# Loading the rows for the scatters in pairs of token tiles, in a two-layer transformer with routed experts

## The chip, the core and the metric

The kernel runs on one core of a Trainium2 chip. The metric is the device time of one execution in microseconds (us); lower is better.

## The reference

The input is x, 4 sequences of 1024 tokens with 256 features in float32. Two layers follow. In each, the same normalised rows go to an attention part and a feed-forward part, and both results are added to x:

```python
xn = _layernorm(x)
x = x + L0_attn(xn) + L0_ffn(xn)
xn = _layernorm(x)
x = x + L1_attn(xn) + L1_ffn(xn)
```

Layer 0 has causal softmax attention and a dense ReLU network. Layer 1 has gated attention in groups of 64 tokens with a linear part beside it, and eight experts:

```python
scores = softmax(xf @ Wg.T)
expert_weights, expert_indices = top_k(scores, 2)
g = silu(h1) * h3                  # h1, h3: each expert's own matrices, with a low-rank part
y_e = _lora_out(g, W2, b2, A2, B2)
y = einsum('te,ted->td', gates, y_e)
```

Each of the 4096 tokens uses the two experts with the highest scores, and the kernel computes only those.

## The kernel before, in words

The program has four stages, joined on every engine: layer 0 (to about 465 us), attention of layer 1 for the first two sequences (to about 620 us), the experts for all tokens (to about 970 us), attention of layer 1 for the last two sequences together with the adding of the experts' results. TensorE works in all of them. Tokens are handled in 32 tiles of 128.

**The rows of the experts.** Layer 0 leaves in HBM (xn1_scratch, `scr["xn1"]`) for every token two copies of its normalised row, each followed by the gate of one of its experts: 2 x 257 floats, 2056 bytes for each token. When every token's experts are known, VectorE works out for each token and choice a slot (unit CH, the last of it at L1734), such that the slots of one expert are contiguous, 71 tiles of 128 slots in all. Then the rows must be moved to their slots in slot_rows_scratch (`scr["xs"]`). That takes two steps for each tile of tokens. SyncE loads the tile into one place of `ring` in SBUF, which has RINGS = 4 places of one tile (unit RG, L1303). GpSimd then issues two scatters by index, one for each choice (unit SC, L1347). The semaphore `ring_in` of the place tells GpSimd that the load has landed; the semaphore `moved` of the place, raised by 16 by each scatter that has landed, tells SyncE that the place is free (L1302). So RG:n waits for both scatters of tile n - 4. When all is moved, SyncE loads the slots' rows, six tiles ahead, into xs_ring (unit ML, L1830 to L1833), and the experts' stage begins (units MR, MA, MC, MG, MO for every tile of slots: rows turned, two products, gate, turned again, product out).

**What else stands in the same queues.** The order of units on each engine is written out by hand (ATTENTION_UNITS, L1007), and an engine never departs from it. GpSimd's has the 32 SC, and among them YS:0 to YS:8, each the power -0.5 of one tile's variance (L1339), and LE:0 to LE:2, the three parts of the first expert's matrices (L1783 and L1787; LE:1 stands between SC:26 and SC:27, LE:2 between YS:8 and SC:29). YS:9 and those after it stand behind SC:31. YS:n waits for VectorE's variance (L1679) of the same tile; VectorE's unit YF:n (L1683, L1688) waits for YS:n, finishes that tile's normalised output and adds it to x1b. YF:9 stands right behind OO:15, the last product with the gate (L1668), and ahead of the statistics of tiles 11, 12 and 13 (YS), which the first unit of the experts follows (MR:0, L1989). SyncE's queue has, among its RG: SX:n, which stores four finished tiles of x1b (L1295), and LX:1, which loads the second sequence's residual rows, 1024 KB, into x1b once the first is stored (L1288 to L1290, the load itself at L1166). XB:1 on VectorE (L1650) needs those. AHEAD (L1076) says how many units of the next stage are taken in right behind a unit of this one: on SyncE twelve behind RG:31, which are ML:0 to ML:5 and the first six MT, so SX:2 and SX:3 come behind these.

In the views below, tile names are the program's: `slot_rows_scratch<-ring,slot` is a scatter, `ring<-xn_scratch` a load of the ring, `x1b<-x_scratch` LX, `x_scratch<-x1b` SX, `expert_ring<-experts_scratch` a part of an expert, `rsy<-vey,half` YS.

Of the kernel before, what the change touches and what calls it, by code (L numbers as in the profile page):

```python
# [13 lines left out]
P = 128  # L14
# [251 lines left out]
def layer0(nc, io, keep, scr, psum, ctx):  # L266
# [725 lines left out]
    def bank_last(i):  # L992
# [40 lines left out]
        SC:28 YS:8 LE:2 SC:29 SC:30 SC:31 YS:9 YS:10 YS:11 YS:12 YS:13 YS:14 YS:15  # L1033
    """,
    "sync": """
        LC:0 LC:1 LX:0 LC:2 RG:0 RG:1 RG:2 RG:3 RG:4 RG:5 RG:6 RG:7 RG:8 RG:9 RG:10 RG:11 RG:12 RG:13 RG:14 RG:15
        RG:16 RG:17 RG:18 RG:19 RG:20 RG:21 RG:22 RG:23 RG:24 RG:25 SX:0 RG:26 RG:27 SX:1 RG:28 LX:1 RG:29 RG:30
        RG:31 SX:2 SX:3
    """,
},  # L1040
{
# [44 lines left out]
    "scalar": "GA:15:18",  # L1086
    "vector": "YS:13:1 YS:14:2 YF:11:1 YS:15:4 YF:12:19 YF:13:1 YF:15:2",
    "gpsimd": "YS:10:1 YS:13:1",
    "sync": "RG:31:12",
},  # L1090
{
    "tensor": "MC:70:1",
# [76 lines left out]
def attention(nc, io, keep, scr, psum, half, out, ctx, before):  # L1169
# [39 lines left out]
    if half:  # L1209
        z_in, z_stored = [sem(f"first_half_in{b}") for b in range(NB)], sem("first_half_stored")  # L1210
        added = {n: [sem(f"added_{n}_{t}") for t in range(4)] for n in ("z", "x")}
    else:
        chosen, slots_ready, ranks_ready = sem("experts_chosen"), sem("slots_ready"), keep["ranks_ready"]
        w_in, c_in, row_in = sem("l1_weights_in"), sem("l1_cols_in"), sem("l1_rows_in")
        spread_ready, rowprod, folded = sem("ln1_bias_spread"), sem("l1_bias_products"), sem("l1_folded")
        w_high, w_split, offset_step = sem("l1_weights_high"), sem("l1_weights_split"), sem("head_offsets_step")
        ring_in = [sem(f"ring_in{i}") for i in range(RINGS)]
        moved = keep["moved"]
    x2_b = scr["x2"].rearrange("(b t p) d -> b p t d", p=P, t=TPB)
    out_b = out.rearrange("b (t p) d -> b p t d", p=P)  # L1220
# [37 lines left out]
    def sync(sp):  # L1258
        def unit(un):
# [10 lines left out]
            elif kind == "LC" and n == 1:  # L1270
                for read in dense["probs_turned"]:
                    sp.wait_ge(*read)
                sp.dma_start(turn[:], io["turn"]).then_inc(row_in, 16)
                sp.wait_ge(*dense["rows_weighed"])
                sp.dma_start(wo1[:], io["L1_attn_Wo"].rearrange("(c p) n -> p c n", p=P)).then_inc(keep["late_in"], 16)
            elif kind == "LC" and n == 2:
                sp.wait_ge(*dense["columns_read"])
                sp.wait_ge(*dense["crow_read"])
                sp.dma_start(keep["bias"][:], io["distance_bias"]).then_inc(keep["late_in"], 16)
                sp.wait_ge(*dense["hidden_read"])  # L1280
                sp.dma_start(keep["ln2_w"][:], io["L1_attn_ln2_w"].to_broadcast([P, DIM])).then_inc(keep["late_in"], 16)
                sp.dma_start(keep["ln2_b"][:], io["L1_attn_ln2_b"].to_broadcast([P, DIM])).then_inc(keep["late_in"], 16)
            elif kind == "LX" and (n or half == 0):
                if half == 0 and n == 0:
                    sp.wait_ge(*dense["hidden_read"])
                    dense["x1_rows"](sp, BATCH - 1)
                elif half == 0:
                    for h in range(2):  # L1288
                        sp.wait_ge(stored[h], 16)
                load_rows(sp, keep, scr, "x", half, n, x[n][:])  # L1290
            elif kind == "SX":
                b, rows_of = n // 2, slice(n % 2 * 4, n % 2 * 4 + 4)
                sp.wait_ge(x_ready, T0 + 4 * n + 4)
                to = out_b[b + NB] if half else x2_b[b]
                sp.dma_start(to[:, rows_of, :], x[b][:, rows_of, :]).then_inc(stored[n], 16)  # L1295
            elif kind == "RG":
                if n == 0:
                    for b in range(2, BATCH):
                        dense["stored"](sp, b)
                    sp.wait_ge(*dense["gates_stored"])  # L1300
                if n >= RINGS:
                    sp.wait_ge(moved[n % RINGS], 32 * (n // RINGS))  # L1302
                sp.dma_start(ring[:, n % RINGS, :], scr["xn1"][n * P:(n + 1) * P].rearrange("p k d -> p (k d)")  # L1303
                             ).then_inc(ring_in[n % RINGS], 16)
            elif kind == "LZ":
                if n == 0:
                    sp.wait_ge(*before["rows_out"])
                    before["experts_in"](sp)
                sp.dma_start(zx[:, n, :, :], x2_b[n]).then_inc(z_in[n], 16)
            elif kind == "EN":  # L1310
                for q4 in range(2 * NB):
                    sp.wait_ge(stored[q4], 16 * (half + 1))
                sp.wait_ge(z_stored, 16 * 2 * NB)
            elif kind == "SZ":
                b, rows_of = n // 2, slice(n % 2 * 4, n % 2 * 4 + 4)
                for t in range(4 * n, 4 * n + 4):
                    sp.wait_ge(*all_added("z", t))
                sp.dma_start(out_b[b][:, rows_of, :], zx[:, b, rows_of, :]).then_inc(z_stored, 16)
# [3 lines left out]
    def gpsimd(pool):  # L1322
# [12 lines left out]
        def unit(un):  # L1335
# [5 lines left out]
            elif kind == "SC":  # L1341
                if n == 0:
                    pool.wait_ge(slots_ready, 1)
                    pool.wait_ge(*dense["cleared"])
                pool.wait_ge(ring_in[n % RINGS], 16 * (n // RINGS + 1))
                for k in range(TOPK):
                    nc.gpsimd.indirect_dma_start(out=scr["xs"], out_offset=index(k, n),  # L1347
                                                 in_=ring[:, n % RINGS, k * ROW:(k + 1) * ROW],
# [813 lines left out]
```

## Time and profile before

| | us |
|---|---|
| median of three runs | 1117.2 |
| lowest and highest of them | 1113.53 and 1121.52 |
| the profiled execution | 1116.3 |
| its span, from the first to the last instruction | 1114.6 |
| its mean granted TensorE clock | 0.974 of full speed |
| TensorE busy | 1055.8 (95%) |
| VectorE busy | 781.8 (70%) |
| GpSimd busy | 434.6 (39%) |
| ScalarE busy | 393.5 (35%) |
| loads of the ring: 32 issues of 257 KB | 466.4 to 596.0 |
| scatters: 64 issues | 486.6 to 606.2 |

All times in what follows count from the start of the profiled span. Busy shares are means over the whole of it; what a change in one stage is worth has to be read in that stage. A transfer counts as busy for nobody: its issuing engine goes on at once, and who needs the data waits on a semaphore. An idle time is written in brackets behind the instruction that ended it, with what the profile infers to have released it; "issue" is time in which the engine waited for nothing that the profile shows.

### The profile page before, as it was taken

How to read it: one execution, taken by the hardware profiler on the slowest of the kernel's cores; microseconds unless marked ns; L12 is line 12 of the kernel's file. 1: busy time of each engine (PE TensorE's matmuls, PEld its weight loads, DVE VectorE, ACT ScalarE, POOL GpSimd, SP SyncE). 2: the span in 40 equal slices, each digit the busy share in tenths (PEclk: the TensorE clock that was granted, in tenths of full speed). 3: DMA queues.
4: the chain of work that ended last, by engine and by line, in shares of the span. 5: the costliest groups of instructions: out<-in, count | busy, mean ns of one | idle time of the engine just before them, and what ended most of it. 6: DMA issues, size and time to landing. Idle time of an engine off the chain costs nothing.

```text
span 1114.6 us, 20433 instructions
## 1 busy us (share of the span) xinstructions
PE 1055.8 (95%) x6338; PEld 915.2 (82%) x6338; DVE 781.8 (70%) x1741; ACT 393.5 (35%) x770; POOL 434.6 (39%) x416
## 2 busy tenths in 40 slices
PE   5999999999999996995899899999999999999995
PEld 4899999999999996864677788888888888877874
DVE  5688787878788676754565777777777777764745
ACT  2636463555446363431211222222222222442300
POOL 2846454555447331045575100000011010088886
PEclk8999999999999998897899999999999999999998
DMA  9364672666468346425466446534355252265456
GB/s 272 97 206 130 187 244 101 192 160 202 140 190 205 123 148 185 126 76 171 151 189 214 166 136 223 171 116 142 101 194 166 78 194 58 84 123 86 68 95 141
DMA packets 113780, 168.61 MB, mean 151 GB/s; under 512 B 17296, under 2 KB 87568, under 8 KB 113552
## 3 DMA queue, kind: packets, MB, share of 16 engines
q1 hardware_dynamic: 93328, 120.09, 35.5%
q0 software_dynamic: 20352, 47.23, 15.3%
q8 instruction: 58, 0.95, 0.4%
q14 instruction: 42, 0.34, 0.1%
HBM read 96.14 MB, written 71.14 MB: 150 GB/s over the span
## 4 chain that ended last, share of the span: by engine, by line
PE 87%; DVE 4%; issue 2%; another core or an unknown queue 2%; DMA 2%; SPq 1%; POOL 1%; ACT 0%; DVEq 0%; POOLq 0%; ACTq 0%
PE wide L549 19%; PE wide L1900 17%; PE bank L549 11%; PE bank L1900 9%; PE wide L1398 7%; PE bank L1398 3%; PE bank L1925 3%; PE wide L1458 3%; PE wide L1482 2%; PE bank L1482 2%; PE bank L640 1%; PE bank L1893 1%; PE wide L1471 1%; PE wide L1468 1%
## 5 line engine op out<-in xcount | busy, mean ns | idle before, releaser
L1900 PE MATMUL wide<-expert_ring,xsT 128*128 x642 | 170.5, 401 | 3.1 <-DVE xsT L1989 2.3
L1900 PEld LDWEIGHTS wide<-expert_ring,xsT 128*128 128x128 f32 x642 | 113.3, 188 | 23.4 <-issue 3.9
L1958 ACT ACTIVATE gsT<-bank 128x512 fp32r<-128x512 f32 x71 | 42.5, 599 | 242.3 <-PE bank L1925 242.3
L1783 POOL DMA_DIRECT2D expert_ring<-experts_scratch x24 | 17.3, 720 | 264.7 <-issue 137.6
L2001 DVE TENSOR_TENSOR slots_h<-wide,expert_bias 128x512 f32<-128x512 f32 x71 | 49.1, 691 | 68.0 <-PE wide L1900 67.8
L1347 POOL DMA_INDIRECT slot_rows_scratch<-ring,slot x64 | 69.2, 1081 | 52.0 <-DVE slot L1734 32.0
L532 POOL TENSOR_TENSOR folded_matrix<-fold,folded_matrix 128x512 fp32r<-128x512 f32 x48 | 64.0, 1341 | 42.5 <-ACT folded_matrix L726 39.7
L549 PE MATMUL wide<-xnT,w 128*128 128x512 f32 x234 | 60.3, 399 | 0.0
L1900 PEld LDWEIGHTS bank<-expert_ring,gsT 128*128 128x128 f32 x432 | 56.1, 189 | 3.5 <-issue 0.3
L944 DVE TENSOR_TENSOR hT<-hid,hT 128x512 fp32r<-128x512 f32 x64 | 54.6, 860 | 5.9 <-ACT hid L781 5.1
L549 PE MATMUL wide<-xnT,pT 128*128 128x512 f32 (+2 forms) x288 | 58.6, 348 | 0.0
L529 POOL TENSOR_TENSOR rsa<-vea,half 128x1 f32<-128x1 f32 x32 | 21.3, 666 | 95.3 <-DVE vea L908 94.3
L1900 PE MATMUL bank<-expert_ring,xsT 128*128 x210 | 57.5, 409 | 0.1
L1900 PE MATMUL bank<-expert_ring,gsT 128*128 x432 | 57.3, 281 | 0.1
L1900 PEld LDWEIGHTS wide<-expert_ring,gsT 128*128 128x128 f32 x420 | 54.2, 188 | 3.0
L1989 DVE TENSOR_TENSOR gsT<-bank,gsT 128x512 fp32r<-128x512 f32 x71 | 49.1, 691 | 9.9 <-ACT gsT L1958 0.5
L549 PE MATMUL wide<-w,hT 128*128 128x256 f32 x456 | 55.7, 278 | 0.0
L1330 POOL DMA_INDIRECT first_half<-slot_results_scratch,slot x32 | 51.9, 1622 | 9.2 <-issue 9.2
L1900 PE MATMUL wide<-expert_ring,gsT 128*128 x420 | 55.2, 280 | 0.0
L2010 DVE SCALAR_TENSOR_TENSOR slots_g<-slots_h,xs_ring,slots_h 128x512 f32<-128x512 f32 x71 | 53.4, 752 | 2.5
L549 PEld LDWEIGHTS wide<-w,hT 128*128 128x128 f32 x456 | 54.5, 188 | 0.4
L1330 POOL DMA_INDIRECT x1b<-slot_results_scratch,slot x16 | 26.0, 1626 | 73.4 <-DVE x1b L1650 68.9
(284 smaller groups left out, 2589.1 us busy)
## 6 DMA issues: line engine op xcount, KB each, us to landing
experts_scratch<-folded_matrix SPq DMA_DIRECT2D x24, 1024.0 KB, 5.5
expert_ring<-experts_scratch POOLq DMA_DIRECT2D x24, 1024.0 KB, 6.0
raw<-in_expert_weights SPq DMA_DIRECT2D x24, 512.0 KB, 7.5
xs_ring<-slot_rows_scratch SPq DMA_DIRECT2D x71, 128.5 KB, 2.1
slot_results_scratch<-ys_ring SPq DMA_DIRECT2D x71, 128.0 KB, 2.2
slot_rows_scratch<-zeros SPq DMA_DIRECT2D x23, 385.5 KB, 7.5
ring<-xn_scratch SPq DMA_DIRECT2D x32, 257.0 KB
xn_scratch<-u SPq DMA_DIRECT2D x16, 512.0 KB, 7.8
```

Source lines behind the costliest of these rows:

```text
L532: tt(fold_part(n, 1), fold[:, n % 2, :], fold_part(n, 0), ALU.subtract).then_inc(matrix_ready, 1)
L549: ins = mm(o, stationary(i), moving(j), start=(first and q == 0), stop=(last and q == 2))
L944: tt(hT[:, 1, n % IC, :], hid[:, n % 2, :], hT[:, 0, n % IC, :], ALU.subtract).then_inc(hid_low, 1)
L1330: nc.gpsimd.indirect_dma_start(out=target, out_offset=None, in_=scr["ys"], in_offset=index(k, tile_at), bounds_check=SLOTS - 1, compute_op ...
L1347: nc.gpsimd.indirect_dma_start(out=scr["xs"], out_offset=index(k, n), in_=ring[:, n % RINGS, k * ROW:(k + 1) * ROW], in_offset=None, bound ...
L1398: ins = mm(o, stationary(i), moving(j), start=(first and k == 0), stop=(last and k == 2))
L1482: last = mm(o[:, 0:DIM], oT[:, h % 2, e, n % 4 * P:(n % 4 + 1) * P], wo1[:, e, :], start=(e == 0), stop=(e == EC - 1))
L1900: ins = mm(o, parts[i], moving, start=(first and q == 0), stop=(last and q == 2))
L1958: return nc.scalar.activation(o, i, ACT.Copy)
L1989: tt(flat[1], bank, flat[0], ALU.subtract).then_inc(taken, 1)
L2001: tt(h1[:, j % 2, :], H[j % 2][0], bias(e, 0, HID), ALU.add).then_inc(h1_ready, 1)
L2010: stt(out=g[:, i, :], in0=h1[:, i, :], scalar=xs[:, j % ROUND, DIM:ROW], in1=h3[:, i, :], op0=ALU.mult, op1=ALU.mult).then_inc(g_ready, 1)
```

## The change

The ring keeps its size of four tiles but is filled by pairs: one DMA loads tiles 2n and 2n + 1 into two neighbouring places. There are 16 units RG in place of 32. Each waits for both places' scatters, and one semaphore for each pair tells GpSimd that both tiles have landed. In SyncE's order each pair stands where the second of its tiles stood, except that the pair of tiles 28 and 29 stands ahead of LX:1, where tile 28 stood. The scatters and everything on the other engines stay.

```diff
@@ SyncE's order of units, first half @@
-        LC:0 LC:1 LX:0 LC:2 RG:0 RG:1 RG:2 RG:3 RG:4 RG:5 RG:6 RG:7 RG:8 RG:9 RG:10 RG:11 RG:12 RG:13 RG:14 RG:15
-        RG:16 RG:17 RG:18 RG:19 RG:20 RG:21 RG:22 RG:23 RG:24 RG:25 SX:0 RG:26 RG:27 SX:1 RG:28 LX:1 RG:29 RG:30
-        RG:31 SX:2 SX:3
+        LC:0 LC:1 LX:0 LC:2 RG:0 RG:1 RG:2 RG:3 RG:4 RG:5 RG:6 RG:7 RG:8 RG:9 RG:10 RG:11 RG:12 SX:0 RG:13 SX:1 RG:14 LX:1 RG:15 SX:2
+        SX:3
@@ AHEAD @@
-    "sync": "RG:31:12",
+    "sync": "RG:15:12",
@@ attention @@
-        ring_in = [sem(f"ring_in{i}") for i in range(RINGS)]
+        ring_in = [sem(f"ring_in{i}") for i in range(RINGS // 2)]
@@ sync, kind RG @@
-                if n >= RINGS:
-                    sp.wait_ge(moved[n % RINGS], 32 * (n // RINGS))
-                sp.dma_start(ring[:, n % RINGS, :], scr["xn1"][n * P:(n + 1) * P].rearrange("p k d -> p (k d)")
-                             ).then_inc(ring_in[n % RINGS], 16)
+                i, pair = 2 * n % RINGS, slice(2 * n * P, (2 * n + 2) * P)
+                if 2 * n >= RINGS:
+                    for at in (i, i + 1):
+                        sp.wait_ge(moved[at], 32 * (2 * n // RINGS))
+                sp.dma_start(ring[:, i:i + 2, :], scr["xn1"][pair].rearrange("(t p) k d -> p t (k d)", p=P)
+                             ).then_inc(ring_in[i // 2], 16)
@@ gpsimd, kind SC @@
-                pool.wait_ge(ring_in[n % RINGS], 16 * (n // RINGS + 1))
+                pool.wait_ge(ring_in[n % RINGS // 2], 16 * (n // RINGS + 1))
```

## Rows read from the trace of the kernel before

**Rows 1.** The page, part 4: the chain that ended last, by engine.

```profile
PE 87%; DVE 4%; issue 2%; another core or an unknown queue 2%; DMA 2%; SPq 1%; POOL 1%; ACT 0%; DVEq 0%; POOLq 0%; ACTq 0%
```

**Rows 2.** Windows: busy us (xcount) of PE, PEld, DVE, ACT, POOL; clock, DMA share, GB/s.

```profile
500.00:520.00 20.00, 7.37 (x30) 5.52 (x30) 5.01 (x9) 2.37 (x5) 12.03 (x12) 0.76 0.66 190
```

**Rows 3.** Waits of GpSimd, 480 to 625 us: total, times, longest.

```profile
POOL slot_rows_scratch L1347 <- issue: 18.5, 62, 0.7
```

**Rows 4.** Timeline of GpSimd, 486 to 558 us: start, us, instruction [idle before].

```profile
488.56 1.01 POOL L1347 DMA_INDIRECT slot_rows_scratch<-ring,slot  x1 [0.31 <-issue]
...
491.14 0.97 POOL L1347 DMA_INDIRECT slot_rows_scratch<-ring,slot  x1 [0.30 <-issue]
...
514.87 0.97 POOL L1347 DMA_INDIRECT slot_rows_scratch<-ring,slot  x1 [0.30 <-issue]
521.25 1.01 POOL L1339 TENSOR_TENSOR rsy<-vey,half 128x1 f32<-128x1 f32 x1 [5.41 <-DVE vey L1679]
...
557.75 0.94 POOL L1339 TENSOR_TENSOR rsy<-vey,half 128x1 f32<-128x1 f32 x1 [7.61 <-DVE vey L1679]
```

**Rows 5.** Timeline of SyncE, 491 to 497 us: the loads of tiles 4 and 5.

```profile
491.25 0.32 SPq L1303 DMA_DIRECT2D ring<-xn_scratch  x1
...
496.63 0.32 SPq L1303 DMA_DIRECT2D ring<-xn_scratch  x1
```

**Rows 6.** The page, part 6: DMA issues, count, KB each, median us to landing.

```profile
expert_ring<-experts_scratch POOLq DMA_DIRECT2D x24, 1024.0 KB, 6.0
...
xs_ring<-slot_rows_scratch SPq DMA_DIRECT2D x71, 128.5 KB, 2.1
...
ring<-xn_scratch SPq DMA_DIRECT2D x32, 257.0 KB
```

**Rows 7.** Line L1166, SyncE's six loads of 1024 KB (rows of x1 and of xn).

```profile
DMA to landing us min/median/max: 6.1/7.5/8.9
```

**Rows 8.** Timeline of GpSimd, 574 to 608 us: SC:23, SC:26, LE:1, SC:27, YS:8, SC:29, SC:31.

```profile
574.50 0.98 POOL L1347 DMA_INDIRECT slot_rows_scratch<-ring,slot  x1 [0.30 <-issue]
...
581.62 0.98 POOL L1347 DMA_INDIRECT slot_rows_scratch<-ring,slot  x1 [0.30 <-issue]
...
583.88 0.77 POOL L1783 DMA_DIRECT2D expert_ring<-experts_scratch  x1
...
586.28 0.98 POOL L1347 DMA_INDIRECT slot_rows_scratch<-ring,slot  x1 [0.30 <-issue]
...
594.11 0.56 POOL L1339 TENSOR_TENSOR rsy<-vey,half 128x1 f32<-128x1 f32 x1 [4.28 <-DVE vey L1679]
...
597.58 3.12 POOL L1347 DMA_INDIRECT slot_rows_scratch<-ring,slot  x1 [1.47 <-DMA ring<-xn_scratch]
...
606.17 0.99 POOL L1347 DMA_INDIRECT slot_rows_scratch<-ring,slot  x1 [0.30 <-issue]
```

**Rows 9.** Timeline of SyncE, 578 to 597 us: RG:27, LX:1 and RG:31.

```profile
578.91 0.32 SPq L1303 DMA_DIRECT2D ring<-xn_scratch  x1
...
583.83 0.37 SPq L1166 DMA_DIRECT2D x1b<-x_scratch  x1
...
596.01 0.32 SPq L1303 DMA_DIRECT2D ring<-xn_scratch  x1
```

**Rows 10.** Timeline of VectorE, 597 to 615 us: XB:1, OO:15, YF:9, MR:0.

```profile
597.47 2.29 DVE L1650 TENSOR_TENSOR x1b<-x1b,ln_b 128x2048 f32<-128x2048 f32 x1
...
603.97 0.69 DVE L1668 TENSOR_TENSOR oT<-wide,gT 128x512 f32<-128x512 f32 x1 [1.06 <-issue]
607.81 0.48 DVE L1683 SCALAR_TENSOR_TENSOR y<-y,mvy,ln_w 128x256 f32<-128x256 f32 x1 [3.15 <-issue]
...
614.78 0.41 DVE L1989 TENSOR_TENSOR xsT<-bank,xsT 128x256 fp32r<-128x256 f32 x1
```

**Rows 11.** Timeline of TensorE, 500 to 520 us: the two longest idle times.

```profile
507.29 3.44 PE L1482 MATMUL bank<-wo,oT 128*128 128x256 f32 x8 [6.17 <-issue]
...
519.69 2.93 PE L1398 MATMUL wide<-wv,uT 128*128 128x512 f32 x6 [4.71 <-DVE uT L1619]
```

## The prediction, made before the changed kernel was run

> **What bounds the kernel now.** I read the page's chain first: TensorE holds 87% of it [rows 1], so a change on SyncE and GpSimd counts only where it makes TensorE wait, or ends a wait. Then I looked for where the changed loads stand. They feed the 64 scatters, which GpSimd issues from 486.6 to 607.2 us. The stretches there show TensorE busy, with one exception: from 500 to 520 us it worked 7.37 of 20 us [rows 2]. Next, the waits of GpSimd over those 120 us: 62 of its 64 scatters came after a gap put down to "issue", 18.5 us in all, the longest 0.7 [rows 3]. So the present ring of four single tiles almost never makes a scatter wait. The timeline says what does set GpSimd's pace. A scatter takes 0.97 to 0.98 us and the next one starts 0.30 later, so two tiles (four scatters) take 4 x 1.28 = 5.1 us. And GpSimd waits for VectorE: 5.41 us before YS:0, 7.61 us before YS:4 [rows 4], 4.28 us before YS:8 [rows 8]. These idle times are cushions: a scatter that is late ahead of one of them costs nothing. Last, who waits for GpSimd. VectorE sat 3.15 us before YF:9 at 607.81 us, which needs YS:9, and YS:9 stands in GpSimd's queue right behind the last scatter, started at 606.17 us. From there VectorE is busy nearly without a pause up to the first tile of the experts (L1989, 614.78 us) [rows 8, 10]. So the end of the last scatter, 607.16 us, is on the path that sets the end, and delay there is passed on one to one. If it comes sooner, at most those 3.15 us can be won.
>
> **Part 1, sixteen issues instead of thirty-two.** A load's issue takes 0.32 us of SyncE [rows 5]: 16 x 0.32 = 5.1 us less on a queue that mostly waits for scatters to land. Bytes are the same. On the path that is worth nothing, since no scatter but SC:29 ever waited for a load.
>
> **Part 2, the ring now turns by pairs.** Before, the load of tile n waited for the scatters of tile n-4, while GpSimd had three other tiles, 3 x 2.56 = 7.7 us of work. Now the load of a pair waits for the last scatter of the pair two back, and only one pair, 5.1 us, covers it. What has to fit in there are two latencies. From the end of a tile's last scatter to the load it frees: tile 0's ended at 489.57 and its load went out at 491.25, 1.7 us; tile 1's ended at 492.11, its load at 496.63, 4.5 us [rows 4, 5]. I take 2.8, near the middle of these ends. The load itself: the trace gives no landing for these 257 KB. A read of 128.5 KB landed in 2.1 us, one of 1024 KB in 6.0 [rows 6]; a straight line between them makes 2.7 us for 257 KB and 3.8 for the pair's 514 KB. Ends for the pair: 2.1, and the 8.9 us that the slowest read of 1024 KB on SyncE's queue took [rows 7]. So a pair costs 2.8 + 3.8 = 6.6 us against 5.1 of cover: GpSimd stalls 1.5 us, and, because the other pair meanwhile catches up, at every second pair. With the low ends (1.7 + 2.1 = 3.8) it never stalls; with the high ones (4.5 + 8.9 = 13.4) it stalls 8.3 us.
>
> The Trainium skill (DMA: Bandwidth & Descriptors, the section on the anatomy of one DMA from GpSimd's queue) fits a transfer's time as about 2.0 us plus its bytes over 436 GB/s. By an estimate from that page a pair of 0.53 MB would land after 3.2 us instead of my 3.8, and the stall would be 0.9 instead of 1.5; the row with 128.5 KB in 2.1 us agrees with it, the one with 1024 KB in 6.0 lies above its 4.4. My sum doesn't use it.
>
> **Where the stalls fall.** First stretch, SC:0 to SC:10: the pairs at SC:4 and SC:8 stall, together 3.0 us, and GpSimd then waits 5.41 us for VectorE anyway [rows 4]. Nothing. Second, SC:11 to SC:17: one stall, ahead of the 7.61 us [rows 4]. Nothing. Third, SC:18 to SC:28: the pair at SC:22 stalls. Here TensorE's neighbours store and load much else, so SC:26 stalls more: tile 23's last scatter ended at 575.48, its load went out at 578.91, 3.4 us [rows 8, 9]; with a start 0.8 later and 4.5 us of loading beside the stores of x1b, SC:26 starts at 584.2 instead of 581.62, 2.6 late. LE:1, one of the first expert's three parts, 1024 KB, stands between SC:26 and SC:27 and goes out 2.6 late too. SC:28 ends at about 592.7, before YS:8 at 594.11 [rows 8]. The cushion takes the stall on GpSimd, but not what has happened to the DMAs.
>
> **The last pair.** SC:29 came at 597.58 after 1.47 us of waiting for its load [rows 8]. That load stood in SyncE's queue behind LX:1, a load of 1024 KB issued at 583.83 [rows 9]. In the new order tile 29 comes with 28, ahead of LX:1, and that wait goes: SC:29 starts at 596.1. What is late next is tiles 30 and 31. Their load now waits for both tile 26 and tile 27. Tile 27's last scatter ended at 587.26 and it was landed only by 596.01, 8.7 us later, behind LE:1's transfer in GpSimd's queue [rows 8, 9]. With LE:1 2.6 us and LX:1 about 2.1 us later, I put that at 598.3. The load then runs beside LE:2 (issued from 594.7): between the 3.8 of a quiet pair and the 7.5 of the median read of 1024 KB on this queue [rows 7], and I take 5.2, nearer the quiet end, as LE:2's transfer is partly done by then. It lands at 603.5. SC:29, whose first scatter took 3.12 us behind LE:2, would have been through by 600.8. So SC:30 starts at 603.5 instead of 602.3, and SC:31 ends 5.1 us later, 608.6 instead of 607.16: **1.5 us later**. Bounds: if tile 27 lands at 596.0 as now and the load takes 3.8, SC:30 starts at 600.8, the end is 605.9, 1.2 us sooner; if tile 27 lands at 598.3 and the load takes 7.5, the end is 610.9, 3.8 later.
>
> **The store and load moved among the pairs.** SX:0 and SX:1 follow pairs that go out when the second of the old tiles did, so they keep their place in time. LX:1 goes out at about 585.9 instead of 583.83. XB:1 on VectorE needs it at 597.47 [rows 10]; with the slowest 8.9 us [rows 7] and up to 2 us behind the pair in front it lands by 596.8. Nothing, but with only 0.7 us over in the worst case. YS:5, YS:6 and YS:7 move by 0.8 us with the scatters around them; VectorE does their YF later than that. The first loads of the experts' rows wait for SC:31 as before, and what they feed on VectorE comes after YF:9, so they add nothing of their own.
>
> **The sum.** 1116.3 us (span 1114.6 and 1.7 around it) + 1.5 = 1117.8. The median of the runs shown is 0.9 above the profiled execution, so I forecast **1118.7 us**. Those runs lie between 1113.5 and 1121.5, about 4 to either side, so a measurement tells from no change only what is over 1%, 11 us. With the bounds -1.2 and +3.8 and that scatter the forecast's own range is 1112 to 1126.
>
> **Rival A, the tail gains.** Without the wait for tile 29, and with fewer issues, the last pair is ready in time: SC:31 ends 1.2 us sooner, at best by the whole 3.15 us that VectorE waited [rows 10]. That gives 1117.2 - 1.2 to - 3.15, about 1115. For it: the wait that goes was the only one for a load. Against it: the load of 30 and 31 waits for tile 27, as late as ever. The Trainium skill (same page, Rules for kernel authors) would have many small transfers made into large ones; it speaks for this rival, but here such time is saved off the path. Chance 0.2.
>
> **Rival B, slower.** The place is the pair ring at SC:22, SC:26 and SC:30; the mechanism, that with two buffers each congested load is uncovered. It decides when landing plus load passes 5.1 us by more than the cushions. With 4.5 us for the scatters and 7.5 (the median read again) for the load, each stall is 12.0 - 5.1 = 6.9 us; three of them are 20.7, less the 4.28 us cushion before YS:8: 16.4, so 1117.2 + 16.4 = 1134. Half of that still makes 1125. For it: at 587 us a landing took 8.7. Against: a load seldom meets that much traffic. Chance 0.12.
>
> **Rival C, the hole at 500 us changes.** TensorE idled 6.17 us before 507.29 and 4.71 before 519.69 [rows 11], just while 22 scatters and their loads ran without a pause. I can't name its cause. If it comes from the density of the DMAs, and the stalls thin them out, most of 10.9 us would go: 1118.7 - 10.9 = 1108; it could as well grow. Chance 0.08.
>
> **How the numbers follow.** Forecast 0.6, A 0.2, B 0.12, C 0.08. The range runs from 1109, which leaves out the better part of C, to 1129, which holds the milder half of B. Faster by over 1% (below 1106) takes more than C alone gives, so 0.06; slower by over 1% (above 1128) is most of B and a growing hole, 0.12; within 1% the rest, 0.82.
>
> **What would show each step right or wrong.** Sixteen issues of 514 KB. GpSimd waiting for "ring" before SC:4, SC:8, SC:22, SC:26 and SC:30, and for no odd tile; if such waits are absent my latencies are too long, if they exceed 3 us each, too short. YS:0 still waiting for VectorE. SC:29 straight behind LE:2. The last scatter ending within 606 to 611 us, and VectorE's wait before YF:9 changed by the same amount. Wrong would be a TensorE idle elsewhere than at 600 to 625 us that the profile puts down to GpSimd, or a hole at 500 to 520 us of another size.

## The result, and the profile after

| | before | after |
|---|---|---|
| median of nine runs each, us | 1117.2 | 1108.4 |
| lowest and highest of them | 1113.53 and 1121.52 | 1104.95 and 1110.31 |
| the profiled execution | 1116.3 | 1110.31 |
| its span | 1114.6 | 1108.6 |
| ratio after/before, with its 95% interval | | 0.9913 [0.9898, 0.9927] |

The change saves 8.8 us of the medians, 0.9%. I had forecast 1.5 us more, not 8.8 less; 1108.4 lies just below the range of 1109 to 1129. In the profiled executions 6.0 us are saved, and all of it before the experts' stage: its first unit MR:0 started at 614.78 us before [rows 10] and starts at 608.64 now, and what follows comes 6 us sooner to the end. (Lines of the code behind the diff have moved by one: L1348 is now the scatter, L1304 the load.)

The page of the kernel after, part 4 (the chain that ended last, by engine) and part 6 (the loads of the ring). They answer to [rows 1, 6]:

```profile
PE 79%; DMA 6%; issue 6%; DVE 4%; POOL 3%; SPq 1%; DVEq 0%; ACT 0%; POOLq 0%
...
ring<-xn_scratch SPq DMA_DIRECT2D x16, 514.0 KB
```

The loads are what the change says: 16 of 514 KB. And TensorE holds 8 points less of the chain, DMA 4 more: a stretch is now set by transfers, which says that the change costs something too. Windows show both sides. Columns as in [rows 2], of the kernel after:

```profile
500.00:520.00 20.00, 20.00 (x104) 16.46 (x103) 13.91 (x27) 5.91 (x12) 13.49 (x13) 1.00 0.51 160
...
580.00:600.00 20.00, 10.44 (x48) 7.89 (x47) 5.12 (x7) 0.69 (x1) 9.88 (x11) 0.74 0.79 257
```

From 500 to 520 us TensorE works all 20 us, where it worked 7.37 [rows 2]: the hole is gone. From 580 to 600 us, where TensorE had no pause before, it now works 10.44 of 20, at a mean granted clock of 0.74. Comparing the same product in both traces, TensorE was 16.4 us ahead of the old kernel at 521 us, 14.8 at 530, 21.7 at about 540, 18.4 at 576, and 6 at the end of the stage. It had been 0.5 us behind before 500. So 16.9 us came from the hole at 500 us and 6.9 from a second one, which is shown below, and 21.7 less 6.1, or 15.6 us, went back behind them; 1.5 us had gone back between the two.

Where they went is in the waits of GpSimd, 480 to 625 us (total, times, longest), which answer to [rows 3]:

```profile
POOL slot_rows_scratch L1348 <- DMA ring<-xn_scratch: 20.2, 6, 7.3
POOL slot_rows_scratch L1348 <- issue: 18.1, 57, 1.8
```

Before, one scatter waited for a load, 1.47 us. Now six do, for 20.2 us, and the last for 7.3. The 1.75 us before SC:8, which this view puts down to "issue", are a seventh: among those who waited for the tile `ring` the profile lists GpSimd with 22.0 us in 7 places. GpSimd's timeline, kernel after, SC:4, SC:8, YS:0, SC:14, SC:29 and SC:30, the last scatter; it answers to [rows 4, 8]:

```profile
501.19 1.55 POOL L1348 DMA_INDIRECT slot_rows_scratch<-ring,slot  x1 [3.44 <-DMA ring<-xn_scratch]
...
513.46 1.23 POOL L1348 DMA_INDIRECT slot_rows_scratch<-ring,slot  x1 [1.75 <-issue]
...
521.09 0.59 POOL L1340 TENSOR_TENSOR rsy<-vey,half 128x1 f32<-128x1 f32 x1
...
537.06 0.98 POOL L1348 DMA_INDIRECT slot_rows_scratch<-ring,slot  x1 [5.13 <-DMA ring<-xn_scratch]
...
586.49 1.06 POOL L1348 DMA_INDIRECT slot_rows_scratch<-ring,slot  x1 [0.30 <-issue]
...
596.17 0.98 POOL L1348 DMA_INDIRECT slot_rows_scratch<-ring,slot  x1 [7.31 <-DMA ring<-xn_scratch]
...
600.03 0.98 POOL L1348 DMA_INDIRECT slot_rows_scratch<-ring,slot  x1 [0.30 <-issue]
```

Every stall stands ahead of an even tile. YS:0 no longer waits for VectorE: it waited 5.41 us before [rows 4], since VectorE sat in the hole. The last scatter ends at 601.01 instead of 607.16. SyncE's timeline, 577 to 590 us (start, us), has the reasons of the last stall; it answers to [rows 9]:

```profile
577.12 0.36 SPq L1304 DMA_DIRECT2D ring<-xn_scratch  x1
577.57 0.44 SPq L1165 DMA_DIRECT2D x1b<-x_scratch  x1
...
589.03 0.36 SPq L1304 DMA_DIRECT2D ring<-xn_scratch  x1
```

Tile 27's last scatter ended on GpSimd at 581.06, and the load of the last pair goes out at 589.03, 8.0 us later; the load itself takes until SC:30 at 596.17. The chain of waits has the same stretch as follows (start, us, what), and from 557 us to MR:0 nothing in it is work of TensorE:

```profile
580.08 8.89 DMA slot_rows_scratch<-ring,slot
589.03 6.37 DMA ring<-xn_scratch
```

VectorE's timeline, kernel after: YS:8's input, XB:1, YF:9 and MR:0. It answers to [rows 10]:

```profile
584.88 0.15 DVE L1680 TENSOR_SCALAR vey<-mvy 128x1 f32<-128x1 f32 x1 [6.14 <-POOL rsy L1340]
591.17 2.29 DVE L1651 TENSOR_TENSOR x1b<-x1b,ln_b 128x2048 f32<-128x2048 f32 x1 [6.14 <-DMA x1b<-x_scratch]
...
601.66 0.48 DVE L1684 SCALAR_TENSOR_TENSOR y<-y,mvy,ln_w 128x256 f32<-128x256 f32 x1 [5.26 <-POOL rsy L1340]
...
608.64 0.41 DVE L1990 TENSOR_TENSOR xsT<-bank,xsT 128x256 fp32r<-128x256 f32 x1
```

VectorE would have been at each of these places 5 to 6 us sooner. From the last scatter on everything is as before: YF:9 starts 0.6 us behind its end, MR:0 7.0 us after YF:9 in both kernels.

**Who was late in the hole.** [Rows 11] put TensorE's 6.17 us before 507.29 down to "issue". The engines beside it say more. TensorE, ScalarE and VectorE of the kernel before, timelines:

```profile
497.69 2.99 PE L1398 MATMUL wide<-uT,wg 128*128 128x512 f32 x12
```

```profile
514.07 0.69 ACT L1567 ACTIVATE gT<-wide,cols 128x512 f32<-128x512 f32 x1 [17.32 <-remote]
```

```profile
506.34 0.69 DVE L1668 TENSOR_TENSOR oT<-wide,gT 128x512 f32<-128x512 f32 x1 [5.65 <-remote]
```

and ScalarE of the kernel after, the same gate:

```profile
499.94 0.69 ACT L1568 ACTIVATE gT<-wide,cols 128x512 f32<-128x512 f32 x1 [2.66 <-PE wide L1399]
```

This gate on ScalarE needs the first six of the twelve products of L1398. In the kernel before they were through at 499.31 (all twelve by 500.68), and the gate starts at 514.07, 14.8 us later. "Remote" means only that the profile finds no releaser in time, but the trace also keeps the moments at which TensorE's semaphore went up. In the kernel after that was 499.86, 0.02 us behind the end of the same six products, and the gate followed at 499.94. In the kernel before it was 513.99. So what ScalarE waited for was the signal; the work had been done as far as the profile can tell, which models the ends of matmuls.

GpSimd's scatters before ran from 486.6 to 515.8 us without a gap of more than 0.7 us. Single signals of TensorE came through inside this row, at 506.24 for VectorE and at 513.99 for the gate; those left came together from 518.23 to 518.55, 2.4 us behind its end.

**A second hole.** The prediction took the stretch from 500 to 520 us for the only exception; it was not. From 540 to 560 us TensorE of the kernel before worked 16.17 us of 20, at a mean granted clock of 0.83, and ScalarE has the same kind of wait there:

```profile
551.27 0.69 ACT L1556 ACTIVATE r<-wide,cols 128x512 f32<-128x512 f32 x1 [10.55 <-remote]
```

GpSimd had just issued its second row of scatters, from 534.1 to 550.1 us, with YS:3 inside it at 547.05. Behind it GpSimd waited 7.61 us before YS:4 [rows 4]. The kernel after has no wait there, and its TensorE worked 20 of 20 us from 540 to 560. In another execution of it (group 3 below) ScalarE still waited 5.81 us, "remote", before 551.48.

### The profile page after: what moved, and what is told of

It is laid out like the page before. It is cut to its first block, busy times and chain, and to the rows that moved or that the text cites. A ratio compares the mean times of both kernels' runs of the same rounds, so it can differ in the third digit from the quotient of the medians.

```text
span 1108.6 us, 20431 instructions
## 1 busy us (share of the span) xinstructions
PE 1052.9 (95%) x6338; PEld 912.8 (82%) x6338; DVE 782.5 (71%) x1741; ACT 394.0 (36%) x770; POOL 431.2 (39%) x416
## 4 chain that ended last, share of the span: by engine, by line
PE 79%; DMA 6%; issue 6%; DVE 4%; POOL 3%; SPq 1%; DVEq 0%; ACT 0%; POOLq 0%
PE wide L549 19%; PE wide L1901 17%; PE bank L549 11%; PE bank L1901 9%; PE wide L1399 4%; PE bank L1926 3%; DMA ring<-xn_scratch 2%; DMA slot_rows_scratch<-ring,slot 2%; PE bank L1399 2%; POOL slot_rows_scratch L1348 2%; PE bank L640 1%; PE bank L1894 1%; PE wide L1459 1%; DMA lora<-in_expert_lora 1%; PE wide L1472 1%
## 5 line engine op out<-in xcount | busy, mean ns | idle before, releaser
L1784 POOL DMA_DIRECT2D expert_ring<-experts_scratch x24 | 17.3, 720 | 263.3 <-issue 137.4
L1348 POOL DMA_INDIRECT slot_rows_scratch<-ring,slot x64 | 66.6, 1041 | 70.4 <-DVE slot L1735 32.1
```

## The experiments

Each group ran on one chip, beside its own runs of the kernel before. The two theories of the first group: the hole goes because the pair ring makes GpSimd pause in its first run of scatters; or it goes because there are fewer and larger DMAs.

**Group 1, kernel before 1098.47 us** (29 runs, 1094.87 to 1103.93). The pairs for the first twelve tiles only (RP is a load by pair, RG a single one):

```diff
-        ... RG:0 RG:1 RG:2 RG:3 RG:4 RG:5 RG:6 RG:7 RG:8 RG:9 RG:10 RG:11 RG:12 RG:13 RG:14 RG:15
+        ... RP:0 RP:1 RP:2 RP:3 RP:4 RP:5 RG:12 RG:13 RG:14 RG:15 ...
```

> Tiles 0 to 11 loaded by pairs as in the changed kernel, tiles 12 to 31 one by one as before, with the old order of SyncE. Theory 1 (the gain is the hole of TensorE at 500 to 520 us, which goes when the loads of the first stretch are by pairs; the pair ring afterwards only costs): hole gone, TensorE busy over 18 of 20 us there, and the waits for the ring at SC:14, SC:22, SC:26 and SC:30 that the changed kernel has (5.1, 1.4, 2.1 and 7.3 us) gone, so faster than the changed kernel, about 1098 us (1108.4 less some 10). Theory 2 (the gain comes from the later stretch, from the new place of LX:1 or the fewer issues there): about 1117. Theory 3 (the hole comes and goes by chance of the code's layout, not by the loads): hole there or not, time 1117 or 1098, with no relation to where the pairs are.

1102.88 us, ratio 1.0037 [1.002, 1.0053].

The pairs for tiles 12 to 31 only:

```diff
+        ... RG:0 RG:1 RG:2 RG:3 RG:4 RG:5 RG:6 RG:7 RG:8 RG:9 RG:10 RG:11 RP:6 RP:7 RP:8 RP:9 RP:10
+        RP:11 RP:12 SX:0 RP:13 SX:1 RP:14 LX:1 RP:15 ...
```

> Tiles 0 to 11 one by one as before, tiles 12 to 31 by pairs with the changed kernel's order. Theory 1: the hole at 500 to 520 us is there as before (TensorE busy 7 to 8 of 20 us), and the pair ring's waits come on top of it in the tail, so 1117 to 1121 us. Theory 2: about 1108, as the changed kernel. Theory 3: either.

1105.52 us, ratio 1.0067 [1.0042, 1.0093]. GpSimd's line for SC:30 and TensorE's longest wait behind it:

```profile
590.85 0.99 POOL L1365 DMA_INDIRECT slot_rows_scratch<-ring,slot  x1 [6.67 <-DMA ring<-xn_scratch]
```

```profile
590.87 3.75 PE L1500 MATMUL wide<-wo,oT 128*128 128x256 f32 x8 [9.19 <-DVE oT L1686]
```

The kernel before with single loads, and two pauses of GpSimd, in which it waits until the tile ahead has landed:

```diff
+                if n in (4, 8):
+                    pool.wait_ge(moved[(n - 1) % RINGS], 32 * ((n - 1) // RINGS + 1))
```

> The kernel before with one thing added: GpSimd waits ahead of SC:4 and SC:8 until the scatters of the tile before have landed, some 3 us each; all loads stay one by one. If it is the pause in GpSimd's stream that takes the hole away (theory 1a), the hole is gone and the time is 1098 to 1105 us, without any pair. If it is the merging of the loads (theory 1b), the hole stays and the time is 1117, as the pauses fall before GpSimd's wait for YS:0.

1102.91 us, ratio 1.0029 [1.0008, 1.005].

The waits and the order of the changed kernel (RG:29 stands ahead of LX:1), but each pair by two DMAs of 257 KB:

```diff
+                for at in (n % RINGS, n % RINGS + 1)[:2 - n % 2]:
+                    sp.wait_ge(moved[at], 32 * (n // RINGS))
```

> As the changed kernel in waits and order (no load of a pair before both its places are free), but with two DMAs of 257 KB for each pair, 32 in all, and a semaphore for each place. Theory 1a (pause): the hole is gone as in the changed kernel, 1105 to 1110 us, since GpSimd stalls nearly as long. Theory 1b (merging): the hole stays, 1117 to 1122.

1103.57 us, ratio 1.0046 [1.003, 1.0062].

On this chip TensorE worked all 20 us from 500 to 520 in all four, the second among them, whose first twelve tiles are those of the kernel before. And that kernel took 18.7 us less than the 1117.2 above. In these four traces all 272 signals of TensorE's products between 480 and 600 us stand 0.01 to 0.02 us behind the products' ends, in the second trace beside a row of 22 scatters as in the kernel before. There was no hole for a change to take away, and each of the four made it 0.3 to 0.7% slower. So these runs can't tell the two theories apart. They price the other side: the waits by pairs cost 4 to 7 us here, also where each pair comes by two DMAs. The whole change was not run on this chip.

**Group 2, kernel before 1117.3 us.** First the question that group 1 raised, is it the chip? The kernel before, unchanged:

> The kernel before, unchanged, once more with a profile. The first four runs came out at 1103 to 1106 us beside a kernel before at 1098.5 (it was 1117.2 when the change was measured), and none of their traces has the hole. Theory A (the hole at 500 to 520 us belongs to some sessions of the chip and not to the kernel alone): 1098 us and no hole here, or 1117 with the hole, and the changed kernel's place beside it turns with it. Theory B (the hole belongs to the kernel before): a hole in this trace, TensorE busy under 10 of 20 us there, whatever the time.

1117.52 us, ratio 0.9996 [0.9976, 1.0016]. Windows of it:

```profile
500.00:520.00 20.00, 9.02 (x38) 6.79 (x36) 4.14 (x7) 0.69 (x1) 13.06 (x14) 0.86 0.73 206
```

The hole is here, and ScalarE's gate came at 513.90 after 15.23 us, "remote". The same program takes 1117.5 on this chip and took 1098.5 on the first: it is not the kernel that makes the difference, but the chip, or what differed between the two occasions on it; every chip was used once. Then the changed kernel, unaltered:

> The changed kernel, unchanged, beside the kernel before. Theory A: where the kernel before has no hole (1098 us) the changed one is slower than it, by 5 to 10 us, about 1105 us, since only the ring's longer waits are left (its trace waited 22 us for the ring, the last time 7.3 us); where it has the hole, faster by 9. Theory B: faster by 9 us in every session, about 1090 if the kernel before is at 1098.

1109.34 us, ratio 0.9927 [0.9909, 0.9945]: no hole, and 18.6 us of waits for the ring.

The changed kernel with LX:1 ahead of the pair of tiles 28 and 29, against XB:1's 6.14 us (RP is this run's name for the RG by pair):

```diff
-        ... SX:1 RG:14 LX:1 RG:15 ...
+        ... SX:1 LX:1 RP:14 RP:15 ...
```

> The changed kernel with LX:1 ahead of the pair of tiles 28 and 29 in SyncE's queue. In the changed kernel's trace XB:1 waited 6.1 us for LX:1 and TensorE 9.6 us behind it. If LX:1's place is what costs, 3 to 5 us faster than the changed kernel; if it is the last pair's wait for tile 27's scatters behind the expert's parts, no difference (under 2 us) or slower, as tile 28 comes later.

1110.93 us, ratio 0.9934 [0.9913, 0.9956], beside 0.9927 without it: nothing gained. XB:1 waits no more, but SC:28 now waits 7.36 us for the pair behind LX:1, and the last scatter ends at 602.80. XB:1's wait alone isn't what sets the tail.

The kernel before, with the expert's loads LE:1 and LE:2 moved ahead of the crowded stretch:

```diff
-        SC:16 YS:3 SC:17 YS:4 ... SC:21 YS:5 ... SC:26 LE:1 SC:27
-        SC:28 YS:8 LE:2 SC:29 ...
+        SC:16 YS:3 SC:17 LE:1 YS:4 ... SC:21 LE:2 YS:5 ... SC:26 SC:27
+        SC:28 YS:8 SC:29 ...
```

> The kernel before with LE:1 and LE:2 taken out of the last scatters: LE:1 stands behind SC:17, LE:2 behind SC:21. If the traffic of these two parts of 1024 KB is what holds the landing of tile 27's scatters (8.7 us) and the last loads, the last scatter ends 5 us sooner and the kernel is 3 to 6 us faster than before; if the scatters' issues alone set the end of the stage, within 1 us.

1116.25 us, ratio 0.9994 [0.9978, 1.001]: no difference while the hole is there. From the end of tile 27's last scatter to the load that it frees it still took 7.0 us (7.4 in the kernel before on this chip), so these two transfers aren't what holds it.

**Group 3, kernel before 1118.61 us.** The comparisons of group 1 again, on a chip that has the hole. The changed kernel:

> The changed kernel again, to see it in one more session. Chips differ: on one the kernel before took 1117 us with the hole, on another 1098.5 without it. Theory A: on a chip with the hole 0.992 to 0.993 of the time before; on one without it 1.005 to 1.01, about 1105 us.

1110.35 us, ratio 0.9928 [0.991, 0.9947].

The edit of the second experiment again (single loads up to tile 11, pairs behind them):

> Tiles 0 to 11 one by one, the rest by pairs, for a chip with the hole: theory 1 says the hole stays (TensorE busy 7 to 10 of 20 us at 500 to 520) and the tail's waits hide behind it, 1115 to 1120 us. On a chip without the hole again 1.005 to 1.01 of the time before.

1119.57 us, ratio 1.001 [0.9993, 1.0027], and the hole stays. Windows:

```profile
500.00:520.00 20.00, 10.23 (x41) 7.87 (x40) 4.19 (x7) 0.00 (x0) 13.66 (x14) 0.74 0.73 198
```

The two pauses again, with every load single as before:

> The kernel before with GpSimd's waits ahead of SC:4 and SC:8 for the scatters of the tile before. On a chip with the hole: if the density of the scatters and loads makes it, it goes and the time falls to 1105 to 1110; if only merged loads take it away, 1117. Without the hole again 1.003 of the time before.

1107.38 us, ratio 0.9884 [0.9863, 0.9905]. Windows:

```profile
500.00:520.00 20.00, 20.00 (x107) 16.62 (x106) 14.85 (x28) 4.64 (x9) 10.40 (x10) 1.00 0.50 140
```

Two waits of GpSimd, and nothing of the change, take the hole at 500 us away and gain more than the change did. Pairs that come only later gain nothing. It is a pause in the first run of scatters that pays; larger loads aren't needed for it.

But this kernel has a hole of its own further on. Its windows, and ScalarE's wait:

```profile
560.00:580.00 20.00, 13.66 (x51) 8.94 (x50) 5.37 (x12) 1.97 (x3) 16.02 (x18) 0.83 0.81 242
```

```profile
570.79 0.59 ACT L1520 ACTIVATE lkv<-wide 64x512 f32<-64x512 f32 x1 [16.29 <-remote]
```

GpSimd issued scatters from 551.2 to 576.1 us here, with YS:5, YS:6 and YS:7 among them at 561.29, 564.41 and 567.68: single short operations don't keep such a hole away everywhere.

Is it then the traffic? From tile 4 the loads move 64 of the 514 floats of a token, with the scatters unchanged (so most of the experts' rows are left out):

```diff
+                wide = TOPK * ROW if n < RINGS else 64
+                sp.dma_start(ring[:, n % RINGS, 0:wide], ...
```

> The kernel before with the same 32 issues, but from tile 4 on each load moves only the first 64 of the 514 floats of a token, so the bytes of the loads all but go (the scatters move old rows; the experts' results are wrong, no other work changes). On a chip with the hole: if the loads' bytes beside the scatters make it, the hole is gone and the time is under 1105; if the number of loads or the scatters alone make it, it stays, 1115. On a chip without it: the last load's waits go, 0 to 4 us faster than before.

1124.97 us, ratio 1.0048 [1.0032, 1.0064]. Windows, and TensorE's wait:

```profile
500.00:520.00 20.00, 3.94 (x23) 3.16 (x22) 0.69 (x1) 0.00 (x0) 13.71 (x15) 0.71 0.36 112
```

```profile
522.18 2.05 PE L1483 MATMUL bank<-wo,oT 128*128 128x256 f32 x4 [18.25 <-DVE oT L1669]
```

The DMA share falls to 0.36, from 0.66 to 0.73 in the kernels with full loads, and the hole grows: 3.94 us of work in 20. The bytes of the loads are not the cause. Their number stayed the same; it is ruled out by the two pauses, which kept all 32. What is left, and what the hole at 500 us follows in every trace of groups 2 and 3, is GpSimd's own unbroken row of scatters.

**Group 4, kernel before 1120.22 us** (no trace of it on this chip; the time is that of a kernel with the hole). Must the scatters land for it, or must GpSimd only do something else for a moment? The changed kernel first:

> The changed kernel once more. Two chips gave 0.9927 and 0.9928 of the time before, with the hole in the kernel before; a third, where it took 1098.5 us, has not seen the changed kernel. On a chip of the first kind 0.993; on one of the other kind slower than before, 1.005 to 1.01.

1112.58 us, ratio 0.9923 [0.9897, 0.9949].

The kernel before, with one small operation of GpSimd ahead of each of SC:1 to SC:10, and no wait:

```diff
+                if 0 < n <= 10:
+                    nc.gpsimd.tensor_tensor(keep["spare"][:, n:n + 1], keep["r2"][:, 0:1], keep["half"][:, 0:1], ALU.pow)
```

> The kernel before with one small operation of GpSimd (128x1, some 0.6 us) ahead of each of SC:1 to SC:10. Nothing waits for anything. If any other work between the scatters lets TensorE's signals through, the hole is gone on a chip that has it, 1105 to 1108 us. If the transfers in flight must come to an end first, it stays, 1117 to 1120.

1105.51 us, ratio 0.987 [0.9832, 0.9908]. GpSimd's timeline, windows, and ScalarE's gate of this kernel:

```profile
489.40 1.01 POOL L1350 DMA_INDIRECT slot_rows_scratch<-ring,slot  x1 [0.30 <-issue]
490.42 0.60 POOL L1348 TENSOR_TENSOR spare<-r,half 128x1 f32<-128x1 f32 x1
491.21 1.05 POOL L1350 DMA_INDIRECT slot_rows_scratch<-ring,slot  x1 [0.18 <-issue]
```

```profile
500.00:520.00 20.00, 20.00 (x103) 16.49 (x102) 13.25 (x26) 5.65 (x11) 16.91 (x18) 1.00 0.51 148
```

```profile
500.26 0.69 ACT L1570 ACTIVATE gT<-wide,cols 128x512 f32<-128x512 f32 x1 [2.66 <-PE wide L1401]
```

Ten operations of 0.6 us that compute nothing needed save 14.7 us of the medians: the gate starts at 500.26, 0.1 us behind its products. GpSimd is busier than in the kernel before (16.91 of 20 us where it was 12.03), and its scatters still go out every 1.3 to 1.8 us. So no wait for a landing is needed, and no pause of several us; in this row one short instruction of another kind between two tiles is enough. In the later rows it was not always: YS:3 stands in the row of the second hole, YS:5 to YS:7 in that of the kernel with the pauses. Whether it is the kind or the 0.5 us that it adds, these runs don't tell.

Five such operations (some 3 us) ahead of SC:4 and of SC:8 only:

```diff
+                if n in (4, 8):
+                    for k in range(5):
+                        nc.gpsimd.tensor_tensor(keep["spare"][:, k + n // 8 * 5:k + n // 8 * 5 + 1], keep["r2"][:, 0:1], keep["half"][:, 0:1], ALU.pow)
```

> The kernel before with five such operations ahead of SC:4 and of SC:8, some 3 us each time, without a wait for any landing. The pause is as long as in the kernel with the waits (3.9 and 4.7 us there). If the pause in the issue of scatters is what counts, the hole goes, 1105 to 1109 us; if only GpSimd standing idle lets the signals through, it stays at 1117.

1105.95 us, ratio 0.9891 [0.9843, 0.994]: no hole at 500 us either (20 of 20 us worked). As good as the waits of the same places, so the pauses needn't wait for anything.

The two pauses together with the expert's loads early:

> The two waits ahead of SC:4 and SC:8, all loads one by one, and LE:1 and LE:2 behind SC:17 and SC:21. With the hole gone the tail sets the end of the stage, and the two parts of the expert are what holds its landings: 2 to 5 us faster than the waits alone, 1103 to 1106 us on a chip with the hole; under the kernel before by 0 to 3 us on one without it. If the tail is set by the scatters' issues alone, no more than the waits alone (1107 and 1.003).

1104.94 us, ratio 0.9868 [0.9837, 0.9898], the last scatter ending at 593.9 us. Tile 27's scatters took 6.0 us to free the ring, without an expert's transfer near them.

**Group 5, kernel before 1116.77 us.** The short operations with the expert's loads early:

> The small operation ahead of SC:1 to SC:10 together with LE:1 and LE:2 behind SC:17 and SC:21. On a chip with the hole each took off 1.3% in one way or with the waits; together, if the tail's landings still count, 1102 to 1105 us, 0.985 of the time before; if not, 0.987 as the small operations alone. On a chip without the hole 0.998 to 1.002.

1104.04 us, ratio 0.9889 [0.9871, 0.9907]: not more than the short operations alone had given. The changed kernel beside it:

> The changed kernel in one more session. With the hole in the kernel before 0.992 to 0.993, as three times so far; without it (the kernel before at 1098 us) slower, 1.005 to 1.01.

1111.62 us, ratio 0.9953 [0.9936, 0.9971], with 21.9 us of waits for the ring in seven places, and TensorE idle for 9.33 us before 598.97.

## Why the prediction was wrong

**What bounds the kernel.** The chain, the cushions ahead of YS:0, YS:4 and YS:8, and the last scatter as the point that hands its delay on one to one: the last of these held to 0.1 us (scatter 6.15 sooner, MR:0 6.14 sooner). But "at most those 3.15 us can be won" failed. I had taken VectorE's 3.15 us before YF:9 as the limit of a gain, with all ahead of it in place. The cushions themselves were made by the holes: VectorE was late at YS:0 because of the first and at YS:4 because of the second, which I had not seen ("with one exception" was a misreading: TensorE worked 16.17 us from 540 to 560). With the holes gone all of it moved: SC:20 came at 554.77 instead of 564.30.

**The step that failed: "Rival C, the hole at 500 us changes", put at 0.08 and kept out of the sum.** Its number, 1108, is what came, but by luck: it stands for 10.9 us gained and nothing lost, where 23.8 were gained in two holes and 17.1 went back. I had seen the two idle times [rows 11] and that 22 scatters ran through just then, and wrote that I couldn't name the cause. What I hadn't done was look one engine further. ScalarE had idled 17.32 us for products that TensorE had finished 14.8 us earlier, so the hole stood on a late signal and not on work. My own forecast of stalls ahead of SC:4 and SC:8 put two pauses right into the run of scatters; I costed them "Nothing", because of the cushion behind, and never asked what a pause of GpSimd gives. The reason that I offered for the rival, the density of the DMAs, was wrong as far as it means the traffic: with half the DMA share the hole grew. That the scatters stand so close together is not excluded.

**Part 1** held as far as it could be told: the issues are 0.36 us each now, and what that saves doesn't show. Whether one DMA or two for a pair makes a difference these runs don't tell, since the changed kernel wasn't run beside the one with two.

**Part 2, the pair ring.** Mechanism right, sizes low. The first freed pair: tile 1's last scatter ended at 492.64, its load went out at 496.41 (3.8 us where I took 2.8) and was there at 501.19 (4.8 where I took 3.8). So a pair costs 8.6 us against 5.1 of cover, and SC:4 stalled for 3.44 where I had 1.5. In all 20.2 us in six places (18.6 to 21.9 in six or seven, in four other executions). The Trainium skill's fit for one DMA from GpSimd's queue (DMA: Bandwidth & Descriptors, the anatomy of one DMA) would give 3.2 us for 0.53 MB, as an estimate from that page; the two loads here took 4.8 and more than 6, both beside scatters, so the measurements lie far above it.

**Where the stalls fall.** "None at an odd tile" held. Costing the stalls of the first two stretches at "Nothing" failed: those of SC:4 and SC:8 gained, and once the cushions were gone, those that followed cost. This is the same failed step seen from the other side: the term was put at nothing because of a wait that the stall itself took away.

**The last pair.** Right in its chain: SC:29 straight behind LE:2, the wait for tile 29 gone, tile 27's landing the thing that is late next, behind LE:1. Tile 27's landing took 8.7 before and 8.0 now; the load, 5.2 in my sum, took 6.4 by the chain. "Behind LE:1's transfer" explains little of it: with both parts of the expert moved far ahead the same step took 6.0 to 7.0 us in three kernels. What was wrong is the time of arrival. With the hole, and so YS:8's wait of 4.28 us, gone, SC:29 came at 586.49 instead of 597.58, 11.1 us sooner, and stood there until a load that could only follow tile 27: SC:30 came 6.1 us sooner. 5 of the 11 us went in this one wait.

**"Nothing, but with only 0.7 us over in the worst case" (XB:1).** LX:1 was 13.6 us on its way (577.57 to 591.17), where I had taken 8.9 for the slowest read [rows 7], and XB:1 could have started at 585.03: 6.14 us of wait. The 8.9 was misread. The trace gives a landing for two of the six loads only, 6.1 and 8.9, both issued at 687 us in another stage; LX:1's own semaphore took its last step before XB:1 at 595.88 in the kernel before, 12.0 us after the issue. With 12.0 in place of 8.9 my own check would have come out at 597.9, past the 597.47 at which XB:1 started. Yet putting LX:1 first won nothing: VectorE's next stop, YF:9, needs the last scatter, which set the end.

**Rivals A and B.** A's wait went, and its gain can't be seen beside the rest. B's mechanism was at work at SC:30, with 7.3 us for my 6.9; over the stage 15.6 us went back, close to the 16.4 that I worked out for it. The result is the sum of two rivals that I had weighed one against the other: C's gain, 16.9 at the first hole (larger than the 10.9 us of idle time that I saw, for there were shorter waits beside it, and at the mean granted clock of 0.76 the work also went slowly) and 6.9 at the second, less B's loss. That the ring's waits cost rather than help is also what group 1 says, where there was no hole and the parts of the change lost 4 to 7 us.

**What stays open.** Why a row of scatters holds back signals of TensorE, inside the chip, and whether in fact it holds back the writing of its products, which the modelled ends of matmuls would hide; why it wasn't so on the chip of group 1 (on those of groups 2 and 3 the traces show the hole, on those of groups 4 and 5 only the times speak for it); and why a short operation was enough in the first row and not always in the later ones. How the whole change does on a chip without the hole: its parts were slower there, and slower is what I would expect, but it wasn't run. And whether the tail could be mended with the change kept; of the versions run none with the pair ring came near the single loads with a break (ratios of 0.987 to 0.989 beside 0.991 to 0.995).

**A version that beats both, where the hole is.** The kernel before with the ten short operations: 1105.51 beside 1112.58 of the changed kernel and 1120.22 of the kernel before on the same chip, and 1104.94 for the two pauses with the expert's loads early. The two can't be told from one another by these runs. Neither was run on the chip without the hole, where the pauses alone cost 0.3%.

## What to carry to other kernels

When a critical engine idles "by issue" or "remote", go one engine further, find when the work it waits for was done, and if that was long before, treat the hole as a number in the sum that any edit near it may switch on or off. Coalescing loads makes the ring behind them coarser: count the places that can be in flight, not only the bytes, and price landing plus load against the cover that is left. And an edit is judged on more than one chip: here the same one (two pauses) was 0.3% slower on one and 1.2% faster on another.

## What the runs showed of the hardware

- In the kernel before and in four other traces, on two chips of the experiments (groups 2 and 3), while GpSimd issued 22 indirect DMAs with no other instruction between them (0.97 us each, 0.30 apart), signals of TensorE went up late: 14.7 us behind the products' end in the kernel before, with ScalarE idle for 17.3 us, and 19.2 us in the one with thin loads. Mostly they stand 0.01 to 0.02 us behind it. Single ones came through inside the row, and the last 2.4 us (kernel before) and 3.2 us (thin loads) behind its end. Even the kernel after has one: due at 496.72, it came at 498.95, 1.2 us after GpSimd had stopped for SC:4. This is a coincidence in time over all runs with the hole, and the runs with a break confirm it; the way by which the one holds up the other was not seen.
- In this first row each of the breaks tried freed them: one operation of 0.6 us between two tiles, five in two places, or a wait. Halving the share of the DMA engines didn't. In later rows, which had single operations in them, ScalarE still waited 10.6 us (kernel before, 551.27) and 16.3 us (kernel with the pauses, 570.79).
- On three chips (groups 3 to 5) a break was worth 11 to 15 us of the 1117 to 1120 that the kernel before took there. On two of these no trace with the hole was taken, and it is inferred from the times. The chip of group 1 ran the kernel before in 1098.5 us.
- Late in the stage tile 27's scatters took 7.4 to 9.0 us to free the ring in the kernels with single loads and an expert's 1024 KB just ahead on GpSimd's queue, and 6.0 to 7.0 with the expert's parts moved away; tile 1's took 3.1 to 4.8. So the expert's parts account for little of it; LX:1's 1024 KB on SyncE's queue goes out about then in all of them, which no run took away.
- The granted clock fell with the idle times: a mean of 0.74 in the stretch with 10.44 us of work in 20, and 1.00 in most that were full; the full one right behind the hole, 520 to 540 us of the kernel before, had 0.90.
